# When a batch's row normalising is done inside the next batch's first unit: attention between two mixture-of-experts layers on one Trainium2 core

## The reference, cut to what matters

```python
x = x + 0.5 * ffn(layernorm(x), ...)
x = x + attn(layernorm(x), Wqkv, b_qkv, Wout, b_out)   # 16 heads of 32, causal, ALiBi bias
x = x + 0.5 * ffn(layernorm(x), ...)

def layernorm(x, eps=1e-5):
    return (x - mean(x)) / sqrt(var(x) + eps)          # over the 512 features
```

## Time and profile before

| | |
|---|---|
| time, median of 3 runs | 2904.47 us (2904.09 to 2905.18) |
| profiled execution | 2902.78 us, of which the span is 2901.1 us |
| PE, matmul | 2484.8 us busy (86%) |
| PE, weight load | 1853.8 us (64%) |
| DVE | 1417.7 us (49%) |
| ACT | 1496.0 us (52%) |
| POOL | 1130.9 us (39%) |
| mean granted TensorE clock | 0.954 |

### The profile page before, as it was taken

How to read it: one execution, slowest core, us unless ns; L and a number is a source line. 1 busy time by engine, 2 the same in 40 slices (tenths; PEclk the granted TensorE clock), 3 DMA queues, 4 the chain that set the end, 5 groups by cost and what they waited for, 6 DMA issues and landing times. The chain is left out here.

```text
span 2901.1 us, 67640 instructions
## 1 busy us (share of the span) xinstructions
PE 2484.8 (86%) x13105; PEld 1853.8 (64%) x13106; DVE 1417.7 (49%) x3703; ACT 1496.0 (52%) x3702; POOL 1130.9 (39%) x945
## 2 busy tenths in 40 slices
PE   0219999999999737989989999898599999999994
PEld 0107888888888624646556565564478888888883
DVE  8775555555543234454544545443345454555431
ACT  0216666666665423444534445345366666666552
POOL 3434555555555400111111011121256555655552
PEclk9999999999999968999999899998799999999997
DMA  5426787877864432333323333232377787877545
GB/s 154 141 102 170 181 199 170 186 178 193 199 136 54 52 95 60 96 88 100 86 78 96 97 92 83 84 93 60 117 179 182 181 186 182 194 186 187 92 54 148
DMA packets 185351, 377.86 MB, mean 130 GB/s; under 512 B 38157, under 2 KB 89229, under 8 KB 185010
## 3 DMA queue, kind: packets, MB, share of 16 engines
q0 software_dynamic: 76416, 168.58, 29.9%
q1 hardware_dynamic: 97440, 198.30, 23.0%
q10 hardware_dynamic: 11410, 10.14, 1.2%
HBM read 236.63 MB, written 126.88 MB: 125 GB/s over the span
## 5 line engine op out<-in xcount | busy, mean ns | idle before, releaser
L504 POOL DMA_INDIRECT x_rows<-f_ob,f_it x320 | 515.2, 1610 | 580.1 <-SPq L466 230.4
L554 PE MATMUL f_psg<-f_wh,f_xh 128*128 x1280 | 534.6, 418 | 5.0 <-DVE f_xl L722 2.5
L554 PE MATMUL f_psg<-f_wh,f_xl 128*128 x1280 | 504.3, 394 | 0.0
L554 PE MATMUL f_psg<-f_wl,f_xh 128*128 x1280 | 501.6, 392 | 0.0
L496 POOL DMA_INDIRECT f_xg<-xn_rows,f_it x320 | 356.6, 1114 | 112.4 <-issue 88.0
L1357 DVE CUSTOM_DVE_ANT_0 a_psa<-a_psa,cst 128x384 f32<-128x384 f32 (+3 forms) x512 | 251.3, 501 | 272.1 <-PE a_psa L1133 259.6
L1260 ACT ACTIVATE a_pt<-a_psb 128x256 f32<-128x256 f32 (+3 forms) x512 | 215.9, 435 | 252.1 <-PE a_psb L1186 247.4
L651 ACT ACTIVATE f_ob<-f_pso,f_wcol 128x512 f32<-128x512 f32 x320 | 220.4, 689 | 189.9 <-PE f_pso L568 189.0
L1049 POOL CAST a_cth<-a_ct 128x512 fp32r<-128x512 f32 x32 | 19.5, 610 | 708.8 <-DVE a_ct L1377 708.8
L722 DVE TENSOR_TENSOR f_xl<-f_psx,f_xh 128x512 fp32r<-128x512 f32 x320 | 221.2, 691 | 137.6 <-ACT f_xh L632 137.6
L733 DVE TENSOR_TENSOR f_hl<-f_psh,f_hh 128x256 fp32r<-128x256 f32 x320 | 135.8, 424 | 291.5 <-ACT f_hh L658 290.4
(11 more groups left out here) (197 smaller groups left out, 4340.9 us busy)
## 6 DMA issues: line engine op xcount, KB each, us to landing
f_wraw<-w_in SPq DMA_DIRECT2D x128, 768.0 KB, 7.0
a_stq<-a_qk SPq DMA_DIRECT2D x128, 144.0 KB
a_stk<-a_qk SPq DMA_DIRECT2D x128, 144.0 KB
r_xt<-x_in SPq DMA_DIRECT2D x32, 256.0 KB, 4.5
xn_rows<-r_xo SPq DMA_DIRECT2D x32, 256.0 KB, 2.9
a_xt<-x_rows SPq DMA_DIRECT2D x8, 1024.0 KB, 5.5
a_x<-x_rows SPq DMA_DIRECT2D x8, 1024.0 KB, 5.3
x_rows<-a_x POOLq DMA_DIRECT2D x8, 1024.0 KB, 5.0
```

The lines of the kernel that those rows point to most:

```text
L504: g.indirect_dma_start(x_d, bass.IndirectOffsetOnAxis(it[:, n:n + 1], 0), ob[:, n % OB, :], None, compute_op=ALU.add).then_inc(s_sca[n % O ...
L554: mm = pe.matmul(psg[:, j, :], x[:, j, k, :], w[:, cols], start=(k == 0 and n == 0), stop=(k == DC - 1 and n == 2))
```

## The change

Two things. First, the normalising of a finished batch's rows (four `normed` on DVE) leaves `output` and becomes `finish`, called in unit 0 of the next batch behind maxima 3, 4, 6 and 8; the last batch's stands behind everything. As batch 0 has no batch before it, it is written out ahead of DVE's loop, which now runs over batches 1 to 6. Second, POOL takes the next batch's inverse deviations in front of the split of unit 0's context rather than behind it. What is computed is the same.

```diff
+    DONE_AT = {3: 0, 4: 1, 6: 2, 8: 3}
...
-            self.order = FIRST if self.first else uses(isinstance(b, int))
+            self.order = FIRST if self.first else uses(isinstance(b, int) and b == B - 1)
...
                     for g4 in range(NG):
+                        if g4 == 1 and not last:
+                            inverse(b + 1, 0, s_mom, s_rd)
                         if g4:
                             split_context(b, g4 - 1)
-                        if g4 == 1 and not last:
-                            inverse(b + 1, 0, s_mom, s_rd)
...
-                    v.wait_ge(s_rd2, b * 2 + 2)
-                    for t in range(TB):
-                        if t >= RX:
-                            v.wait_ge(s_n2o[t % RX], stored(b, t % RX) + 16)
-                        elif whole(b):
-                            v.wait_ge(s_n2o[t], stored(b, t))
-                        normed(xn[:, t % RX, :], x2[:, t, :], 1, t).then_inc(s_n2, 1)
+
+                def finish(b, t):
+
+                    if t == 0:
+                        v.wait_ge(s_rd2, b * 2 + 2)
+                    if whole(b) and b == B - 1:
+                        v.wait_ge(s_n2o[t], stored(b, t))
+                    normed(xn[:, t, :], x2[:, t, :], 1, t).then_inc(s_n2, 1)
...
-                    last, bk = whole(b), Bank(b)
+                    last, bk = whole(b) and b == B - 1, Bank(b)
...
+                            if g == 0 and i in DONE_AT and not (whole(b) and b == 0):
+                                finish(b - 1, DONE_AT[i])
...
-                with v.Fori(0, B - 1) as b:
+                batch(0)
+                with v.Fori(1, B - 1) as b:
                     batch(b)
                 batch(B - 1)
+                for t in range(TB):
+                    finish(B - 1, t)
```

## The result

The changed kernel takes 2840.32 us, the median of 4 runs (2838.50 to 2843.01), against 2904.82 for the kernel before: a ratio of 0.9773, 95% interval 0.9762 to 0.9785, so 64.5 us less. The forecast was 2836.3 in a range of 2820 to 2860.

What follows compares the result with a forecast made beforehand. PE sets the pace, pausing behind DVE's waits for GpSimd and then running at half clock. Gains of 39.1 (unit 1), 26.7 (unit 0) and 2.4 (batch 7's unit 0), together 68.2 us, give 2836.3; 8-in-10 range 2820 to 2860.

Steps and rivals of the forecast that it cites:

- Which waits, and that they cost more than their idle time: DVE's 40.5 us of waits for GpSimd cause 14 PE pauses, 50.8 us; half-clock matmuls after each add to the loss.
- the rival's 2858: Rival, chance 0.15: only PE's idle time comes back, 46.6 us, giving 2858; with all norms uncovered, 2868.
- Unit 1: Batches 0 to 6: removing pause and clock loss takes 28.59 to 23.0 us, gain 5.6 each, 39.1 in all.
- not given back: In unit 1, 1.7 us added to the subtraction's 21.3, since ACT and DVE do not return all of it.
- Unit 0, batches 1 to 6: From 26.76 us to the control's 21.71 plus 0.6 for norms: gain 4.45 each, 26.7 in all.
- part 1 of the change: Normalising leaves the batch turn; 1.39 us of issue stays, first maximum at 1236.46, PE's pause 0.2 at most.
- the control of 21.71 us: Unit 0 of batch 0 before the change: no batch turn ahead, no pause, clock 1.00, same statistics; 21.71 us.
- The signs of being wrong: Wrong if the clock falls without those pauses, unit 0 is over 24, or units 2 and 3 grow.
- The slower rival: Chance 0.03: pauses behind norms keep PE at half clock in unit 0, 2928; decides from 32.4 us; control near 36.
- The norms in unit 0: Four norms, 2.0 us, go into DVE's gaps between unit 0's maxima; 0.6 us taken, one norm uncovered.
- GpSimd's order and the moved stores at no cost: Inverse fits GpSimd's 27.09 us idle before the split; stores move 4 to 9 us later, covered; both cost zero.
- What is late next: SP's stack copies keep unit 1 from going below about 22 us; ACT's 1.65 us wait on them grows.

Runs made afterwards that it cites:

- experiment 1: Kernel before with only GpSimd's inverse deviations moved ahead of the context split, norms left at the batch turn: 2863.50 us, ratio 0.9853 to the kernel before.
- experiment 2: Changed kernel with DVE's loop turned, so the jump back falls where DVE waits for PE: 2819.19 us, ratio 0.9708 to the kernel before.
- experiment 4: Turned-loop kernel with four bias-row copies per unit issued by GpSimd instead of SP, its inverse moved ahead of them: 2817.42 us, ratio 0.9696 to the kernel before.

## Why the prediction was right, point by point

- *Which waits, and that they cost more than their idle time.* Right for DVE's waits, fourteen of which went, and for PE's seven pauses in unit 1. At five of the seven batch turns PE's pause shrank from some 3.6 to 1.7 us and did not go. Each kernel that removed pauses gave back more than the pause: 42.9 us for 27.1 in experiment 1; in experiment 2, with five pauses of 1.7 us gone (8.5), the units 0 gave back 16.75. That only idle time returns would have made 2877 and 2832 us there, where 2863.5 and 2819.2 were measured, and the rival's 2858 for the whole change is as clearly off 2840.3.
- *Unit 1.* The term was 39.1 (23.0 us each), the trace shows 200.16 - 156.57 = 43.6 (22.4 each). The mechanism was right, pause and clock together. The 1.7 us that I held back as "not given back" was too careful by 0.6 a unit.
- *Unit 0, batches 1 to 6.* Here the step failed. The term was 26.7, the trace shows 160.56 - 142.95 = 17.6. The step is part 1 of the change: "So the first maximum starts at about 1235.07 + 1.39 = 1236.46 [...] a pause of 0.2 at most." It took the 1.39 us of issue as a fixed gap. It was what was left of a jump of some 3.1 to 3.6 us after the norms had covered 2.00 of it; the change took that cover away. The first maximum came 3.0 us after PE's first score matmul instead of 1.43, PE paused 1.7 us in five turns, and the jump cost 142.95 - 126.20 = 16.75 us in all. I had priced a visible gap at 7 at most and counted nothing. Without the jump the six units took 126.2, a gain of 34.4: more than the term, as the mean unit was 21.03 and not 22.3. That is a second error, of the other sign, and it hid part of the first: the control of 21.71 us was one trace's, and the same unit took 20.41 to 21.64 in the eight others.
- *The signs of being wrong.* Some of them came. PE had waits over 1 us at five batch turns (1.7), and unit 0 was to take about 22.3 at a clock near 1.00, with over 24 as a sign of being wrong: the six took 20.97 to 27.25, 23.8 on average, three of them 24.00 or more, at clocks down to 0.81. By the prediction's own test its account of unit 0 was wrong while its total held.
- *The slower rival.* Half a clock behind short pauses did come, by another cause: not the norms but the jump, and in part of the turns only. The worst unit 0 took 27.25 us, short of the 32.4 from which it would have decided. The rival's "near 36" is not worked out in the prediction: twice the control's 19.9 us of busy matmuls is already near 40.
- *The norms in unit 0.* 0.6 predicted, 0.56 in the changed kernel (20.97 - 20.41), about 0.3 in two later traces: the right size, and no closer than that.
- *Batch 7's unit 0.* 2.4 predicted, 2.6 measured.
- *GpSimd's order and the moved stores at no cost.* Right: the inverse is ready over 10 us ahead, and no wait of PE or DVE on the stores shows. GpSimd itself now waits for the norms ahead of the stores, inside time in which it idled anyway.
- *What is late next.* Wrong. "Unit 1 can't be shorter than about 22 for that reason" named SP's stack copies; experiment 4 took that wait away and unit 1 stayed at 22.4. So "about 22" was close by luck. ACT's wait on them in unit 1 did grow, from 1.65 to 1.97 us, but it lay beside PE's work. It moved no term of the sum.
- *The sum.* 68.2 predicted; the terms measured 43.6 + 17.6 + 2.6 = 63.8 in the traces, and 64.5 by the medians. Two errors of opposite sign, 4.5 too little in unit 1 and 9.1 too much in unit 0, left it 4 us off. That they nearly cancel is luck. The traces also hold 4.4 us of gain in units that the sum leaves out (1.3 in unit 0 of batch 0, 2.0 in unit 1 of batch 7, 1.1 in units 2 and 3) and the 3.5 us lost ahead of attention; both are within what such stretches differ by from trace to trace.

## What to carry to other kernels

A gap before the first instruction behind a loop turn is only what sticks out of the jump; work queued ahead of it covers the rest. Whoever moves that work away has to find the full price first, and can place the jump where the engine waits anyway: turning the loop took another 0.7% off by the ratios, some 19 us, more than a quarter of what the change itself gave. And a wait that an engine shows beside a busy PE (ACT's 42 us on the copies) is not a bound until taking it away has shown so: here 39 us less of it left the time unchanged within the intervals.

## What the runs showed that I had not expected

The jump costs DVE 3.60 us from the start of the last four small instructions ahead of it to the first behind, with those four taking 0.57 themselves. The Trainium skill ("Runtime: NRT & Kernel Launch", Instruction fetch mechanics) says that a taken branch to code outside the prefetched window waits for a fetch. The runs agree that the jump costs and that straight code in its place shows no price, and they give the jump this size. That DVE waits for a fetch in it no run shows.

PE's clock did not answer equally to equal pauses. In the changed kernel, windows of PE after pauses of 1.68 and 1.71 us:

```profile
1562.25:1575.00 12.75, 12.43 (x75) 6.38 (x75) 11.28 (x40) 6.56 (x12) 2.37 (x4) 1.00 0.40 152
1671.05:1684.00 12.95, 12.95 (x49) 7.24 (x50) 8.27 (x28) 5.17 (x8) 2.19 (x4) 0.60 0.39 147
```

After the first the clock stays at 1.00, and unit 0 takes 23.10 us; after the second it is 0.60 over the same stretch, mostly 1.2 GHz, PE gets through 49 matmuls instead of 75, and the unit takes 27.25. So the idle time of such a pause is 1.7 us and what its unit lost against batch 1's 20.97 is between 2.1 and 6.3 us. The five losses sort by the unit's granted clock: 2.1 and 2.3 us at 1.00, 3.0 and 3.4 at 0.93, 6.3 at 0.81. So beyond the pause it is the clock that costs; what decides whether it falls stays open.
